# Attention 0: two maxima of each unit moved from k=1 to k=2, VectorE's order there changed, the maximum split on VectorE

## The reference

```python
c_q = h_t @ W_DQ + b_DQ
c_kv = h_t @ W_DKV + b_DKV
q_c, k_c, v_c = (c_q @ W_UQ + b_UQ), (c_kv @ W_UK + b_UK), (c_kv @ W_UV + b_UV)   # per head, 128
q_r, k_r = (c_q @ W_QR + b_QR), (h_t @ W_KR + b_KR)                               # 32
scores = einsum('bhsd,bhtd->bhst', concat(q_c, q_r), concat(k_c, k_r)) * scale
attn = softmax(scores, axis=-1)
o = einsum('bhst,bhtd->bhsd', attn, v_c)
x = x + o.reshape(b, s, -1) @ W_O + b_O
```

## Time and profile before

| | |
|---|---|
| median of 3 runs | 986.89 us (986.42 to 987.73) |
| profiled execution | 986.89 us, its span 985.1 us |
| TensorE busy | 848.3 us (86%), mean granted clock 0.923 |
| VectorE busy | 587.8 us (60%) |
| ScalarE busy | 519.0 us (53%) |
| GpSimd busy | 330.1 us (34%) |
| maxima, L1649 on VectorE | 256 of 682 ns, 163.4 us |
| maximum products, L1019 on TensorE | 105.8 us |
| score products, L1042 on TensorE | 124.1 us |
| additions, L489 on GpSimd | 128 of about 1280 ns |

### The profile page before, as it was taken

How to read it: one execution, slowest core, us unless ns; L and a number is a source line. 1 busy time by engine, 2 the same in 40 slices (tenths; PEclk the granted TensorE clock), 3 DMA queues, 4 the chain that set the end, 5 groups by cost and what they waited for, 6 DMA issues and landing times.

```text
span 985.1 us, 15083 instructions
## 1 busy us (share of the span) xinstructions
PE 848.3 (86%) x5146; PEld 504.4 (51%) x5146; DVE 587.8 (60%) x1280; ACT 519.0 (53%) x889; POOL 330.1 (34%) x339
## 2 busy tenths in 40 slices
PE   5799999999999865899998535999999999999858
PEld 2354444344343243579987323555655556555436
DVE  6956767767765157653366597657476574754061
ACT  3246566566556642336665211665756656565632
POOL 3326656667557861660240831010202102000000
PEclk9969999999999996899999566899999999999969
DMA  9300000000000000112231200000000000000001
GB/s 332 124 1 1 1 1 1 1 1 1 1 1 1 1 1 0 65 55 62 80 88 51 65 0 1 1 1 1 1 2 1 1 0 0 0 1 1 1 1 43
DMA packets 22634, 24.38 MB, mean 25 GB/s; under 512 B 3591, under 2 KB 20105, under 8 KB 22314
## 3 DMA queue, kind: packets, MB, share of 16 engines
q1 hardware_dynamic: 19896, 17.90, 5.6%
q0 software_dynamic: 2048, 4.20, 1.4%
q10 hardware_dynamic: 626, 1.43, 0.4%
HBM read 14.34 MB, written 9.18 MB: 24 GB/s over the span
## 4 chain that ended last, share of the span: by engine, by line
PE 61%; DVE 21%; ACT 7%; issue 5%; POOL 4%; DMA 1%; ACTq 0%; DVEq 0%; SPq 0%; POOLq 0%
PE ps L1366 8%; PE ps L1418 6%; PE ps L1042 5%; PE ps L1050 5%; PE ps L1392 5%; DVE mx_part L2037 5%; PE ps L1019 4%; ACT rounded L620 3%; PE ps L1058 3%; DVE mx_part L1649 3%; PE ps L1309 3%; DVE cT L1672 2%; POOL xn L489 2%; PE ps L1008 2%; ACT pt L869 2%
## 5 line engine op out<-in xcount | busy, mean ns | idle before, releaser
L1649 DVE TENSOR_REDUCE mx_part<-ps 128x1 f32<-128x512 f32 x256 | 163.4, 682 | 71.5 <-PE ps L1019 70.6
L869 ACT ACTIVATE pt<-ps 128x1024 f32<-128x1024 f32 (+1 forms) x160 | 142.7, 938 | 86.8 <-PE ps L1392 45.8
L677 ACT ACTIVATE pt<-ps 128x512 f32<-128x512 f32 x256 | 140.9, 596 | 82.3 <-PE ps L1042 78.0
L2037 DVE TENSOR_REDUCE mx_part<-ps 128x1 f32<-128x512 f32 (+3 forms) x256 | 138.8, 585 | 37.0 <-PE ps L1370 23.8
L1366 PE MATMUL ps<-rounded 128*128 128x512 f32 (+3 forms) x384 | 143.5, 427 | 12.2 <-DVE mx_part L2037 4.5
L620 ACT ACTIVATE rounded<-ps 32x512 fp32r<-32x512 f32 (+3 forms) x166 | 98.2, 593 | 92.8 <-PE ps L1345 32.2
L1042 PE MATMUL ps<-rounded 100*128 100x512 f32 x256 | 124.1, 496 | 12.3 <-ACT pt L677 11.5
L1019 PE MATMUL ps<-rounded 98*128 98x512 f32 x256 | 105.8, 432 | 10.9 <-DVE rounded L1642 7.6
L1366 PEld LDWEIGHTS ps<-rounded 128*128 128x128 f32 x384 | 73.8, 204 | 76.1 <-DVE mx_part L2037 49.4
L1392 PE MATMUL ps<-rounded 128*128 128x512 f32 (+3 forms) x384 | 104.1, 370 | 8.9 <-ACT pt L869 7.2
L2037 DVE TENSOR_REDUCE mx<-ps 128x1 f32<-128x128 f32 (+3 forms) x128 | 57.1, 487 | 83.5 <-PE ps L1370 82.1
(11 more groups left out here) (252 smaller groups left out, 1278.3 us busy)
## 6 DMA issues: line engine op xcount, KB each, us to landing
wm<-in_wm SPq DMA_DIRECT2D x1, 4896.0 KB, 15.6
kstage<-to_experts SPq DMA_DIRECT2D x10, 256.0 KB
of_experts<-pt SPq DMA_DIRECT2D x10, 256.0 KB, 2.4
to_experts<-kstage SPq DMA_DIRECT2D x4, 512.0 KB, 4.2
wm<-in_experts SPq DMA_DIRECT2D x1, 1028.0 KB
x<-in_x SPq DMA_DIRECT2D x4, 256.0 KB, 6.1
out<-x SPq DMA_DIRECT2D x4, 256.0 KB, 2.3
to_experts<-kstage SPq DMA_DIRECT2D x2, 448.0 KB, 5.4
```

The source lines that it names most:

```text
L677: nc.scalar.activation(pt0(k, i), ps[:, ST0_BANKS[i % 2], :], ACT.Exp, scale=SCALE0).then_inc(exp_done, 1)
L869: nc.scalar.activation(pt[:, 4 * (t % 2) + 2 * g:4 * (t % 2) + 2 * g + 2, 0:w], ps[:, ST1_BANKS[2 * g]:ST1_BANKS[2 * g] + 2, 0:w], ACT.Exp ...
L1649: v.tensor_reduce(mx_part[u % 2][:, o:o + 1], ps[:, max_bank(u, n), :], AX_X, ALU.max).then_inc(max_done, 1)
L2037: v.tensor_reduce(dst, ps[:, banks[s % len(banks)], o:o + w], AX_X, ALU.max).then_inc(max1_done, 1)
```

## The change

The table `max_slots` moves two of the next unit's pieces from k=1 to k=2 for units from 1 on, and puts the two that are left at k=1 in its second half (places 2 and 3). VectorE takes pieces and reciprocals in another order at k=1 and k=2. The split of the maximum, which ScalarE and GpSimd made for units from 1 on, is made by VectorE for all units, with a two-operand maximum in place of the reduction that joins the halves, and a wait for the transposes of the last unit; `negative_max`, `low_max`, the tile `mx_neg` and its semaphore are gone. Places and order in unit 0 are as before. In the changed file these lines stand 18 up: L1019 is L1001, L1042 L1024, L1050 L1032, L1058 L1040, L1008 L990, L1642 L1624, L1649 L1631, L1654 (joining) L1636, L1672 L1654.

```diff
 def max_slots(u):
-    here = [(0, 4), (1, 4), (2, 2), (3, 5), (4, 5)] if u else [(0, 5), (1, 4), (2, 4), (3, 5), (4, 5)]
+    here = [(0, 4), (1, 2), (2, 4), (3, 5), (4, 5)] if u else [(0, 5), (1, 4), (2, 4), (3, 5), (4, 5)]
...
+    if u:
+        slots[1] = [None, None] + slots[1]
...
-            def low_max(u):
-                pool.wait_ge(m_split, u * 2 + 1)
-                pool.wait_ge(mx_neg_ok, u)
-                nc.gpsimd.tensor_tensor(mstage[:, :, :, NZ + 1], mx_neg[:].rearrange("p (h t) -> p h t", h=HP),
-                                        mstage[:, :, :, NZ].bitcast(F32), ALU.subtract).then_inc(m_split, 1)
...
-                    if j == 1 and u + 1 < U0:
-                        low_max(u + 1)
...
-            def negative_max(u):
-                m = mx[u % 2][:, 0:HP * TS]
-                act.wait_ge(mx_ok, u + 1)
-                act.wait_ge(m_turn, u * 4)
-                nc.scalar.activation(mstage[:, :, :, NZ], m.rearrange("p (h t) -> p h t", h=HP), ACT.Copy,
-                                     scale=-1.0).then_inc(m_split, 1)
-                act.wait_ge(m_split, u * 2)
-                nc.scalar.activation(mx_neg[:], m, ACT.Copy, scale=-1.0).then_inc(mx_neg_ok, 1)
...
-                        if u + 1 < U0 and k == 5 and i == 1:
-                            negative_max(u + 1)
...
             def split_max(u):
                 pp, n = u % 2, HP * TS
                 dve.wait_ge(max_done, (u + 1) * NMX0)
-                v.tensor_reduce(mx[pp][:, 0:n], mx_part[pp][:, 0:2 * n].rearrange("p (c n) -> p n c", c=QH), AX_X,
+                v.tensor_tensor(mx[pp][:, 0:n], mx_part[pp][:, 0:n], mx_part[pp][:, n:2 * n],
                                 ALU.max).then_inc(mx_ok, 1)
-                if u:
-                    return
                 dve.wait_ge(mx_ok, u + 1)
                 m = mx[pp][:, 0:n].rearrange("p (h t) -> p h t", h=HP)
+                if u:
+                    dve.wait_ge(m_turn, u * 4)
...
                 pieces(0, 0, 1, 2, 3, 4)
                 z_lo_at(0)
-                pieces(1, 0, 1, 2, 3, 4)
+                pieces(1, 0, 1, 2)
                 rden(0)
+                pieces(1, 3, 4)
+                rden(1)
                 z_lo_at(1)
-                rden(1)
                 pieces(2, 0)
                 rden(2)
-                pieces(2, 1, 2, 3, 4)
+                pieces(2, 1)
                 rden(3)
+                pieces(2, 2, 3, 4)
```

More of the change, by code:

```diff
@@ L242, in build @@
         gathered = xnT[:].rearrange("p (t k n) -> p t k n", t=TS, k=TOPK)
-        mx_neg = sb("mx_neg", [P, HP * TS])
         mx = [sb(f"mx{i}", [P, HG * TS]) for i in range(2)]
@@ L321, in build @@
         v_ones = sem("v_ones")
-        z_mm, z_hi, z_lo, mx_neg_ok, mx_ok, mx1_ok = map(sem, ("z_mm", "z_hi", "z_lo", "mx_neg_ok", "mx_ok", "mx1_ok"))
+        z_mm, z_hi, z_lo, mx_ok, mx1_ok = map(sem, ("z_mm", "z_hi", "z_lo", "mx_ok", "mx1_ok"))
         s_mm, max_done, m_split, m_turn, m_rows = map(sem, ("s_mm", "max_done", "m_split", "m_turn", "m_rows"))
```

## The result

The changed kernel takes 993.54 us, median of 4 runs (993.18 to 994.7), beside 987.31 for the kernel before (4 runs, 986.42 to 988.39). The ratio is 1.0064 [1.0047, 1.0082]: **+6.2 us, slower**, clear of the noise. The forecast was 986.1 us in a range of 980.0 to 989.5, so time and sign are both missed. Timed once more later, it gave 994.87 beside 987.69.

The account below looks back on a forecast made before the run. TensorE was taken to bound the first attention, waiting 1.18 us at k=1 of units 1 to 6. Edits 1 and 2 -0.6, k=7 -1.8 and clock +1.6 summed to -0.8: 986.1 us, range 980.0 to 989.5.

Parts of the forecast that it names:

- Edit 1: Two maxima leave the first half of k=1: its 1.18 us wait goes, 1.92 us leave this place per unit.
- Rival E: The maximum would still wait for the low half in its new place: near 986.9 us, chance 0.02.
- Edit 2 at full clock: Maxima enter k=2: three new waits, 1.7 us, give the gain back; with edit 1 net 0.1 us gained per unit.
- Rival D: VectorE's run from maximum a to e is longer, 0.3 us more per unit: 989.5 us, chance 0.09.
- The clock: TensorE's clock after the new waits: five units of six low where four were, one more, +1.6 us.
- B: Low clock in all six units after the new waits: 987.7 us, chance 0.26.
- C: Short waits lower the clock less: two of six units low gives 981.3 us, none 978.1; chance 0.20.
- Edit 3 on VectorE: Split of the maximum on VectorE: some 0.4 us added, covered by 0.82 us idle, so nothing; uncovered 2.8 us.
- Edit 3 on GpSimd: GpSimd's additions start earlier, TensorE's idle at k=7 of units 0, 3 and 4 goes: 1.8 us gained.
- The signs by which the prediction was to be found wrong: Three waits in k=2 and k=3 much shorter than 1.7 us together, or the clock staying up.

Follow-up runs that it names:

- after: The changed kernel, all three edits on the kernel before: 993.54 us beside 987.31, ratio 1.0064.
- the kernel with GpSimd's order changed: Kernel before, with GpSimd's bias addition and query copy ahead of the low part of the maximum: 986.37 us, ratio 1.0003.
- the gated split: Kernel before with the split on VectorE, GpSimd waiting for its end before the bias addition and query copy: 986.63 us, ratio 0.9986.
- the split alone: The first experiment: kernel before with only the split of the maximum moved to VectorE: 990.7 us beside 986.68, ratio 1.0046.
- the places alone: The second experiment: kernel before with the maxima moved and VectorE's new order, split left on ScalarE and GpSimd: 990.06 us, ratio 1.0034.
- the timed kernel with the reduction: Changed kernel with the maximum's halves joined by the old reduction, not the two-operand maximum: 987.79 us, ratio 1.0007.
- after again: The changed kernel, nothing altered, timed once more beside later runs: 994.87 us, ratio 1.0065 to the kernel before.

## Why the prediction was wrong, point by point

**Edit 1: right.** The wait of 1.18 at k=1 is gone in all six units and nothing takes its place there. Rival E is refuted.

**Edit 2 at full clock: right.** Waits of 0.3, 0.7 and 0.7 were worked out; 0.42, 0.70 and 0.71 came. The net of -0.1 us per unit came as -0.03. Rival D, a longer run of VectorE at this place, did not happen. What the prediction had not asked is what the places give with the old order of VectorE: 0.74 us less a unit.

**The clock: right in count, the term not settled.** Five of the six units are low after the new waits, as taken (unit 1 is not), in both profiled executions of after. But the four of before, from which the term counts, are those of one execution: with the same wait of 1.18 at k=1 the kernel with GpSimd's order changed and the gated split have six, the split alone three. So whether +1.6 is the right size isn't shown; the places alone gave +3.4 [+1.0, +5.8], which holds the +1.0 of edits 1 and 2 with this term only at its edge. Neither B (six low) nor C (two or none) came in after, though six did in the timed kernel with the reduction. The observation about streams that cycle through PSUM banks (the Trainium skill, "TensorE: Matmul & The Clock Gate", section "A second HAM failure mode: psum-queue depth-cycling") is borne out in so far as waits of at most 0.71 us on bank rotation were followed by the low level.

**Edit 3 on VectorE: the step that failed.** The prediction said "So nothing": 0.4 us added against 0.82 of cover. The 0.19 us of the earlier trace rows was read at 48.4 us, where GpSimd runs nothing, and in units 3 and 4 of before the copy started behind L507, so after the split. Two things were not put side by side. The maximum changed "from a reduction to a two-operand form of the same size", which was taken as the same cost; and "GpSimd no longer waits for k=5" was booked as a gain without asking what then runs beside what. Held by GpSimd, the three took 3.40 us in units 3 and 4 in place of 0.65, so 2.75 more against the 0.82 of cover. Each time TensorE waits 1.68, which with its restart costs 1.9, and then pays 1.3 for the low clock, less the 0.53 that k=7 gives back: +2.6 per unit, +5.2 us. Without the collision the step was right: the gated split gives 0.9986 [0.997, 1.0002].

**Edit 3 on GpSimd: the trace as forecast, the time not shown.** The idle at k=7 is gone: with its restart 0.74 us in unit 0 and 0.53 in each of units 3 and 4, 1.8 together as worked out. But the reordering alone gave 1.0003 [0.9983, 1.0022] against the 0.9982 of -1.8 us, which is just outside. And it is this very freedom of GpSimd that makes the collision.

**The sum with what was measured**: -0.2 (edits 1 and 2), +1.6 (clock), +5.2 (units 3 and 4, their k=7 included), -0.7 (k=7 of unit 0) = +5.9, of +6.2. The closeness is partly luck: between the two traces the start-up and unit 0 together gave -2.3 us and the later phases, which are not edited, +1.8, of which the sum has only the -0.7. Nor is the failed step the whole miss: with the collision taken away the change measured +1.5 [+0.2, +2.9] where -0.8 was forecast. The gated split alone (-1.4) is near its forecast of -1.8 and the places alone (+3.4) are not near theirs of +1.0, so these last 2 us point to edits 1 and 2 and the clock; that is argued, not shown.

**The range** was too narrow since no rival had the contention as its mechanism; D had VectorE's run longer at another place and at 0.3 us a unit. The signs by which the prediction was to be found wrong looked at edits 1 and 2 alone: the three waits are 1.83 us together and the clock fell, so none of them came up although the time was outside the range.

**Left open.** How often the clock falls in an execution isn't settled by the kernel alone: behind the 1.66 us wait of the split alone the value products took 1.07 us, at full clock, and in that profiled execution units 4 to 6 had no low stretch at all, while the same kernel's median is 4.5 us above before. The first experiment and the second sum to +7.9 by their ratios, where after has +6.2; the intervals of 2.0 and 2.4 us cover that. What decides in an execution which waits are followed by the low level was not tried. Nor was why GpSimd's copy begins 0.84 us ahead of the join in unit 3 and 0.25 in unit 4 of one execution (the first of the reduction), on which the size of a collision hangs.

## What to carry to other kernels

When work moves to VectorE, list what GpSimd runs at that very time, and look at the operands of each VectorE instruction: with two in SBUF, or as a `tensor_scalar`, it waited here for the GpSimd instruction that was running to end, however small it was itself, while a reduction, or an instruction that reads PSUM beside SBUF, did not. A chain of n small dependent instructions then costs n of GpSimd's, so its price is set by the neighbour and not by its size. And when a wait on one engine is removed, ask first what that engine now runs earlier, and beside what; here the cheapest cures were one instruction in another form (7.1 us by the medians) and one wait (about 5).

## What the runs showed of the hardware

- A VectorE instruction of 128x16 with two operands in SBUF, or a `tensor_scalar`, took 0.18 to 0.19 us alone and up to 1.31 (the split alone, unit 4) beside GpSimd's additions, two of which take 2.52. In all the traces every one that was held ended 0.03 to 0.05 us after an instruction of GpSimd. In units 3 and 4 the two engines alternated, instruction by instruction, and GpSimd's were not lengthened (1.04, 2.52). The join as a reduction took 0.19 beside GpSimd's copy.
- Waits of 0.42, 0.70 and 0.71 us close behind one another were followed by the lower clock level in five of six units in after, after again and the places alone, and in three to six units in the other kernels that have them, some of these stretches twice as long. The single one of 1.18 was in four of six (before), six (GpSimd's order, and the gated split) and three (the split alone). With the first two of the three waits alone it was three of six.
- With the six waits of 1.18 at k=1 taken away (7.1 us) and GpSimd's order changed, the time fell by 15.4 us. Of the 14.0 in units 1 to 6, 6.5 are the shorter units at full clock, 6.4 the four low stretches that stood behind the waits and 1.1 the idle at k=7.
